# Memory attention and FFN of one stage: the sine and its sum moved ahead of a pair's work, the next attention's constants spread over steps, a factor 0.6 moved into a copy

## The reference

```python
x = x + _L2_xattn_ref(_layernorm(x), ctx)
x = x + _L2_ffn_ref(_layernorm(x), W1, b1, theta, wr, wi, W2, b2)

def _L2_xattn_ref(query, keys):
    query1, keys1 = 0.4 * query, 0.6 * keys
    attn = softmax(einsum('bqd,bkd->bqk', query1, keys1), axis=-1)
    return einsum('bqk,bkd->bqd', attn, keys1) + keys

def _L2_ffn_ref(x, W1, b1, theta, w_real, w_imag, W2, b2):
    hidden = x @ W1 + b1                                    # 256 -> 1024
    imag = w_imag * sin(theta + hidden * 0.1)
    phase = cos(theta) * w_real + sin(theta) * w_imag
    return relu(hidden + phase * imag * 0.1) @ W2 + b2      # 1024 -> 256
```

## Time and profile before

| what | value |
|---|---|
| median of three runs | 2768.37 us (2766.84 to 2772.7) |
| the profiled execution: device time | 2771.76 us |
| its span, first to last instruction | 2769.9 us |
| granted TensorE clock over the span, mean | 0.934 |
| TensorE busy over the span | 88% |
| VectorE busy, ScalarE busy | 51%, 41% |

### The profile page before, as it was taken

The page is one execution under the profiler, slowest core; times in us unless marked ns, Lnnn a source line. Parts: engine busy times, 40 slices in busy tenths (PEclk is TensorE's granted clock), DMA queues, the critical chain, the costliest instruction groups (busy, mean ns, idle before and its releaser), DMA issues. The chain is left out here.

```text
span 2769.9 us, 47740 instructions
## 1 busy us (share of the span) xinstructions
PE 2430.6 (88%) x18024; PEld 1816.6 (66%) x18024; DVE 1412.6 (51%) x2880; ACT 1142.0 (41%) x2775; POOL 731.0 (26%) x796
## 2 busy tenths in 40 slices
PE   7989789996897979799999799986989898898884
PEld 5767666664676967566664688864555667867762
DVE  5767401114665867421113566655756726326548
ACT  4468432222776635212222333325636534123316
POOL 4556240004554411120004112221101013102247
PEclk9999799998998999799999899997999998998888
DMA  4000451116000000512114100002000022102100
GB/s 176 2 2 2 200 192 46 46 42 224 2 2 20 1 1 2 226 51 96 46 46 161 63 1 1 1 2 90 1 1 1 24 77 70 46 1 80 44 3 31
DMA packets 64685, 147.11 MB, mean 53 GB/s; under 512 B 9726, under 2 KB 42494, under 8 KB 59393
## 3 DMA queue, kind: packets, MB, share of 16 engines
q1 hardware_dynamic: 58318, 127.27, 13.2%
q0 software_dynamic: 6144, 16.79, 1.9%
HBM read 101.42 MB, written 42.60 MB: 52 GB/s over the span
## 5 line engine op out<-in xcount | busy, mean ns | idle before, releaser
L3621 POOL TENSOR_TENSOR l3x_Pn<-l3x_Pn,l3x_fac 128x616 f32<-128x616 f32 (+2 forms) x96 | 70.3, 761 | 309.8 <-DVE l3x_fac L3671 309.8
L1590 DVE TENSOR_TENSOR l1f_work<-l1f_work,l1f_psU 128x512 f32<-128x512 f32 x55 | 37.8, 687 | 189.2 <-PE l1f_psU L1344 189.2
L1997 POOL TENSOR_TENSOR l2a_Pn<-l2a_Pn,l2a_rden 128x1024 f32<-128x1024 f32 x32 | 60.0, 1897 | 265.2 <-DVE l2a_rden L2238 265.2
L1590 DVE TENSOR_TENSOR l0f_work<-l0f_work,l0f_psU 128x512 f32<-128x512 f32 x39 | 26.8, 688 | 187.1 <-PE l0f_psU L1344 133.8
L1451 ACT ACTIVATE l1f_work<-l1f_psG 128x512 f32<-128x512 f32 x55 | 32.8, 597 | 193.7 <-PE l1f_psG L1337 193.7
L1278 POOL DMA_INDIRECT l1f_rows_in_out<-results_by_expert,l1f_row x32 | 30.8, 963 | 286.7 <-DMA results_by_expert<-l1f_rows_in_out 277.3
L1360 PE MATMUL l1f_psY<-l1f_W,l1f_hT 128*128 (+1 forms) x440 | 104.2, 380 | 0.8 <-ACT l1f_hT L1457 0.8
L1278 POOL DMA_INDIRECT l0f_rows_in_out<-results_by_expert,l0f_row x32 | 30.9, 967 | 250.2 <-DMA results_by_expert<-l0f_rows_in_out 240.7
L838 ACT ACTIVATE l1a_att_Pn<-l1a_att_psS,l1a_att_nmx 128x128 f32<-128x128 f32 x256 | 91.7, 416 | 1.7 <-DVE l1a_att_nmx L947 1.7
L838 ACT ACTIVATE l0x_Pn<-l0x_psS,l0x_nmx 128x128 f32<-128x128 f32 x256 | 91.8, 419 | 0.9 <-DVE l0x_nmx L947 0.9
L1360 PEld LDWEIGHTS l1f_psY<-l1f_W,l1f_hT 128*128 128x128 f32 x440 | 80.6, 190 | 16.6 <-issue 8.2
(11 more groups left out here) (779 smaller groups left out, 7155.7 us busy)
## 6 DMA issues: line engine op xcount, KB each, us to landing
l1f_W<-in_l1f_w SPq DMA_DIRECT2D x9, 1536.0 KB, 19.7
l0f_W<-in_l0f_w SPq DMA_DIRECT2D x8, 1536.0 KB, 24.4
l3x_K<-keys SPq DMA_DIRECT2D x16, 512.0 KB, 5.6
values<-l1f_W SPq DMA_DIRECT2D x11, 512.0 KB, 3.2
rows_by_expert<-zeros SPq DMA_DIRECT2D x1, 4992.0 KB, 24.9
l0f_rows_in_out<-rows_by_expert SPq DMA_DIRECT2D x39, 128.0 KB, 2.1
results_by_expert<-l0f_rows_in_out SPq DMA_DIRECT2D x39, 128.0 KB, 1.7
l1f_rows_in_out<-rows_by_expert SPq DMA_DIRECT2D x39, 128.0 KB, 2.2
```

The lines of the kernel that those rows point to most:

```text
L1590: nc.vector.tensor_tensor(h[n % 2], sg[n % 2], psU[:, :], ALU.mult).then_inc(h_ready, 1)
L1997: nc.gpsimd.tensor_tensor(part, part, rden[b % 2][:, 8 * u:8 * u + 8].unsqueeze(2).to_broadcast([P, 8, P]), ALU.mult)\
L3621: nc.gpsimd.tensor_tensor(v, v, fac[n % 3][:, s * HH:(s + 1) * HH].unsqueeze(2).to_broadcast([P, HH, SEG[s]]), ALU.mult)\
```

## The change

Five edits in `memory_attention_and_ffn` and in the constants' function:

1. ScalarE's `sine(k-1)` stands right behind `turns(k)`, ahead of `relu(k-2)` and of the pair's and group's work.
2. VectorE's `combine(k-1)` stands right behind `fraction(k)`, ahead of that work.
3. The factor 0.6 on the reciprocals (L2603) is dropped; ScalarE's copy of the transposed weights scales by 0.6.
4. The constants of the next attention are cut up: the ten identity sums one to a step from 24 to 33, the rest in three pieces at steps 35, 37 and 39.
5. The 16 `bn_aggr` that closed the stage are issued one to an `add`, one batch late; the last is left for the end.

```diff
@@ def take_pT(q)
-            nc.scalar.activation(PT[q % 2][:, :], banks(q)[1][:, T2:2 * T2], ACT.Copy).then_inc(pt_ready, 1)
+            nc.scalar.activation(PT[q % 2][:, :], banks(q)[1][:, T2:2 * T2], ACT.Copy, scale=0.6).then_inc(pt_ready, 1)
@@ scalar, for k in STEPS
             if 0 <= k < NK:
                 turns(k)
+            if 0 <= k - 1 < NK:
+                sine(k - 1)
             if 0 <= k - 2 < NK:
                 relu(k - 2)
...
                 exps(pair_at(k, 2))
-            if 0 <= k - 1 < NK:
-                sine(k - 1)
@@ def read_memory(q)
             step.do(nc.vector.reciprocal(r[:, :], den[q % 2][:, :]))
-            step.do(nc.vector.tensor_scalar(r[:, :], r[:, :], 0.6, None, ALU.mult))
@@ vector
+        def moments(b):
+            dve.wait_ge(x_ready, min(b + 2, NB))
+            step.wait()
+            step.sig(nc.vector.bn_aggr(out=G.mv[:, b * 2:b * 2 + 2], in_=st6[:, b * 6:(b + 1) * 6]))
+
         for k in STEPS:
             if 0 <= k < NK:
                 rounded(k)
                 fraction(k)
+            if 0 <= k - 1 < NK:
+                combine(k - 1)
             if pair_at(k, 0) is not None:
                 normalise(pair_at(k, 0))
...
-            if k == NK + 2:
-                kernel_attention_constants(nc, G, dve, step)
-            if 0 <= k - 1 < NK:
-                combine(k - 1)
+            if NK - FC <= k < NK - FC + 10:
+                add_identity(nc, G, dve, step, k - (NK - FC))
+            if k == NK + 3:
+                split_high(nc, G, dve, step)
+            if k == NK + 5:
+                split_low(nc, G, dve, step)
+            if k == NK + 7:
+                join_parts(nc, G, dve, step)
             if 0 <= k - DOWN - 2 < NK and k % 2 == 0:
-                add((k - DOWN - 2) // 2)
+                b = (k - DOWN - 2) // 2
+                add(b)
+                if b >= 1:
+                    moments(b - 1)
         step.wait()
-        for b in range(NB):
-            step.sig(nc.vector.bn_aggr(out=G.mv[:, b * 2:b * 2 + 2], in_=st6[:, b * 6:(b + 1) * 6]))
+        moments(NB - 1)
         step.wait()
```

More of the change, by code:

```diff
@@ L2698, in kernel_attention_weights, with add_identity @@
     G.l3a, G.ahead = R, R.loads
-def kernel_attention_constants(nc, G, dve, step):
+def add_identity(nc, G, dve, step, i):
     R = G.l3a
[L2704 to L2715, removed]
+    c, k = divmod(i, 5)
+    if i == 0:
+        dve.wait_ge(R.loaded, 16 * len(R.loads))
+    wd = R.w[:, c * 5 * D + k * D + c * P:c * 5 * D + k * D + (c + 1) * P]
+    step.sig(nc.vector.tensor_tensor(wd, wd, G.ident[:, :], ALU.add))
@@ new lines, in split_high, with split_low @@
+def split_high(nc, G, dve, step):
+    R = G.l3a
+    step.do(nc.vector.tensor_copy(R.partb[:, :], R.bias3[:, :]))
+    step.do(nc.vector.tensor_copy(R.part[0][:, :], R.partb[:, :]))
+    step.do(nc.vector.tensor_tensor(R.part[2][:, :], R.bias3[:, :], R.part[0][:, :], ALU.subtract))
+def split_low(nc, G, dve, step):
+    R = G.l3a
+    step.do(nc.vector.tensor_copy(R.partb[:, :], R.part[2][:, :]))
+    step.do(nc.vector.tensor_copy(R.part[1][:, :], R.partb[:, :]))
+    step.do(nc.vector.tensor_tensor(R.part[2][:, :], R.part[2][:, :], R.part[1][:, :], ALU.subtract))
+    step.do(nc.vector.tensor_copy(R.diag[:, :].rearrange("p (h e) -> p h e", h=HC), G.headmask[:, :].unsqueeze(2).to_broadcast([P, HC, HD])))
@@ L2716, in kernel_attention_constants, with join_parts @@
+def join_parts(nc, G, dve, step):
+    part, b3 = G.l3a.part, G.l3a.b3
     step.do(nc.vector.tensor_scalar(part[0][:, :], part[0][:, :], G.ident[0:3, 0:1], None, ALU.mult))
     step.do(nc.vector.scalar_tensor_tensor(part[0][:, :], part[1][:, :], G.ident[0:3, 1:2], part[0][:, :], ALU.mult, ALU.add))
-    step.do(nc.vector.scalar_tensor_tensor(b3[:, :], part[2][:, :], G.ident[0:3, 2:3], part[0][:, :], ALU.mult, ALU.add))
-    step.do(nc.vector.tensor_copy(diag[:, :].rearrange("p (h e) -> p h e", h=HC), G.headmask[:, :].unsqueeze(2).to_broadcast([P, HC, HD])))
+    step.sig(nc.vector.scalar_tensor_tensor(b3[:, :], part[2][:, :], G.ident[0:3, 2:3], part[0][:, :], ALU.mult, ALU.add))
```

## The result

| | before | after |
|---|---|---|
| median of the runs taken together | 2767.9 us (4) | 2748.9 us (4: 2742.87 to 2751.32) |
| ratio after to before, 95% interval | | 0.9918, 0.9902 to 0.9934 |
| profiled execution, its span | 2771.76, 2769.9 | 2742.87, 2741.1 |
| the stage, from its first root (`l2xf_std`) to the next stage's first `xn` | 197.0 | 177.1 |

The kernel became 0.82% faster, 22.7 us of 2767.9 by the ratio (18.3 to 27.1); the two medians differ by 19.0. The forecast was 2748.5. The spans of the two profiled executions lie 28.8 apart. The changed stage holds 19.9 of that; most of the rest is the fourth layer's cross attention, whose code is the same and which takes 462.1 in the one trace and 453.9 in the other.

A forecast was written before the change was run, and what follows sets the result against it. TensorE bounds the stage from step 16; before that and in the tail it waits on VectorE and ScalarE. 6.2 + 4.3 - 0.1 + 8.9 + 0.8 = 20.1 us, from 2768.37 to 2748.5, range 2743 to 2759.

The forecast's parts named there:

- Steps 0 to 7: First eight steps of the stage: sine and sum go earlier, turns(8) moves from 1937.1 to 1930.9, 6.2 us won.
- Steps 8 to 15: Next eight steps: TensorE carries to turns(14), then ScalarE; 34.1 against 38.4, 4.3 us won.
- Steps 16 to 23: TensorE-bound steps: the root's load comes 0.4 late for the transposes, the rest 0.3 shorter; -0.1 us.
- rest 0.3 shorter: Steps 16 to 23: the rest 0.3 us shorter, against the root's load 0.4 late.
- The tail: After turns(31): eleven downs at 1.72 each, the last add starts at 2051.6 instead of 2060.49; 8.9 us won.
- The `bn_aggr`s: Stage end: sixteen bn_aggr become two, 1.17 becomes about 0.35 with a wait between; 0.8 us won.
- The product: VectorE's product with 0.6, held 1.27 us by GpSimd's add; in the step count, at most 2.5 us on the path.
- A held kt or ft: VectorE's kt and ft beside GpSimd's bias adds: bounds 0 and 8.5 us, taken as 0 on the path.
- the holds lain bare: Rival: GpSimd's holds of kt and ft reach the path, 20.1 - 8.5 = 11.6 us won, 2756.8; chance 0.10.
- The scaled copy: ScalarE's copy scaled by 0.6: bounds 0 and 0.3 us each, four on the path; taken as 0.
- The clock: Rival: up(8) spared half speed, 2745.7 us, or more half-clock places, up to 2753.5; within the forecast's 0.66.
- The end time: Whole kernel: forecast 2748.5 us against 2768.37, or the profiled execution's 2771.76 becoming 2751.7.

The follow-up runs named there:

- The constants' kernel: The kernel before with only the next attention's constants cut up and spread over steps; stage 189.0 us against 197.0, ratio 0.9947 (0.9932 to 0.9961).
- the order: The kernel before with only sine and its sum moved ahead of the pair's work; stage 186.5 us against 197.0, ratio 0.9946 (0.9927 to 0.9966).

## Why the prediction was right, by its steps

- *Steps 0 to 7, 6.2 forecast*: 6.5. The chain of single events came within 0.15: turns(3) at 1907.01 (1907.1), turns(4) 1910.42 (1910.5), turns(6) 1917.28 (1917.3), `up(8)` 1927.04 (1927.0), turns(8) 1930.85 (1930.9). Leaving `up(8)` at half clock was right for this trace. One reading was off without harm: between turns(0) and turns(1) no `up` is at half clock (`up(1)` takes 1.99 before and 1.88 after); the 3.4 us are four `weigh` matmuls and that `up`.
- *Steps 8 to 15, 4.3*: 4.2. TensorE carried it to turns(14), 22.4 behind turns(8) (22.35 forecast), and ScalarE from there.
- *Steps 16 to 23, -0.1*: -0.6, the term furthest off. The root's table load behind sine and relu did what was said and more: the transposes of `xm` wait 1.05 for it instead of 0.54, and `up(24)` waits 0.23 for `xmT`, which hadn't waited. The "rest 0.3 shorter" that was to pay for it didn't come, since TensorE is the bound there (32.44 busy before, 32.42 after).
- *The tail, 8.9*: 8.8 by the start of the last add. *The `bn_aggr`s, 0.8*: 0.6 when undone; the last two take 0.49, not 0.35. The terms were forecast at 20.1 in sum and measured at 19.5. The stage fell by 19.9; the other 0.4 lies ahead of turns(0), where the prediction had no term and where the three traces of the changed kernel spread by as much themselves.
- *The product*: none of its rows is left, and the sums behind it aren't held. Its price, up to 2.5 in the count, is 2.7 measured in place, in one trace.
- *A held kt or ft, 0 on the path*: right for the path (0.0 when the overlap was removed); "up to 1.4 later" was too high, 0.41 for each `ft`, and `kt` wasn't held at all (0.42). The Trainium skill (GPSIMD Engine Reference, Key points) names the contention, and the trace agrees with it for `ft`: an instruction with two SBUF inputs beside a GpSimd add took 1.10 instead of 0.69, and the two adds 1.98 instead of 1.41. It didn't turn into time. (Had the holds lain bare, 20.1 less 8.5 would have left 11.6, as the rivals have it, not 11.5.)
- *The scaled copy, 0*: its row is 0.36, as unscaled. *The clock*: its rival, `up(8)` spared, didn't come in this kernel.
- *The end time*: 2748.5 against 2748.9, but that closeness is partly luck. The sum itself gives 2768.37 less 20.1, 2748.3; the profiled execution was forecast at 2751.7 and took 2742.87. The profiled pair differs by 28.8 where the sum says 20.1, and untouched code alone spreads by 13 us from trace to trace (below), so a match within 0.4 is chance. The stage is what the prediction rested on, and it is what the runs bear out.

Two things stay open. The constants' kernel is faster by 0.53% as a whole (11 to 20 us) where its stage shows 8.0. The others lean the same way: the order 15.5 against 10.5, the changed kernel 22.7, 25.0 and 21.9 against some 20, these within their intervals. Before has one trace, so where the rest lies can't be said. And whether the 4.1 to 5.5 us that the copy of `xmT` takes off the stage arrive in the whole, where one set of runs shows nothing and the other 5.7.

## What to carry to other kernels

Where one engine serves a tight loop and a slower, periodic one, try the loop's link first in each step: here the periodic work had slack of several steps and the loop had none, and the move was worth 10.5 us of a stage of 197. It has a limit: the one piece of periodic work that the next `up` waited for, the copy of `xmT`, had to go ahead of the sine again. Look in the groups' rows for an instruction with a tiny operand and a median far above its minimum; its price is another engine's instruction. After a reordering, the wait that is left names the next edit: here the row `[3.01 <-ACT l2xf_xmT L2493]`, worth 4.1 to 5.5 us of the stage.

## What the runs showed of the hardware that was not expected

- The overlap of VectorE's `ft` with GpSimd's adds costs both: 0.69 became 1.10 and 1.41 became 1.98. The two adds apart, with `ft` at 1918.72 for 1.10 between them:

```profile
1918.43 0.84 POOL L2551 TENSOR_TENSOR x<-x,l2xf_b 128x256 f32<-128x256 f32 x1 [3.48 <-DVE l2xf_xm L2626]
```

```profile
1919.24 1.17 POOL L2551 TENSOR_TENSOR x<-x,l2xf_b 128x256 f32<-128x256 f32 x1
```

The three end one after the other, at 1919.27, 1919.82 and 1920.41, and by the same 0.55 and 0.59 in the other two groups. That fits each having stood still until the one before was done, as the two-element product did, which ended 0.02 behind GpSimd's add; it doesn't look like two engines going slower side by side. No run here separates the two further.
- The granted clock's half-speed spots wander between executions of the same code. `up(8)` took 3.05 us in one execution of the kernel with xmT's copy first and 1.98 in the other, on another chip, behind the same wait of 0.69. The fourth layer's cross attention, untouched in all, took between 453.6 and 467.0 us in fourteen traces, and both ends come from one chip. In the trace of before and of after:

```profile
2219.00:2681.10 462.10, 413.27 (x3776) 343.91 (x3776) 214.63 (x513) 128.15 (x172) 100.16 (x119) 0.92 0.16 46
```

```profile
2198.30:2652.20 453.90, 407.70 (x3776) 338.35 (x3776) 214.58 (x512) 128.02 (x172) 100.13 (x119) 0.94 0.16 47
```

The same 3776 instructions keep TensorE busy for 5.6 us more at a clock of 0.92 than at 0.94, with VectorE, ScalarE and GpSimd alike to 0.13: most of the 8.2 us between them is clock, and a change of that size can only be judged by its own stage and by many runs.
